# Two experts' 64-row remainders put into one shared 128-row tile in a tokeniser, attention and expert kernel

## The reference

```python
cap = int(CAP_FACTOR * B * S / E)          # 1.25 * 2048 / 8 = 320
idx = argmax(softmax(t @ Wr));  pos = rank of the token within its expert
kept = pos < cap
disp[idx * cap + pos] = t                  # (8 * 320, 256), kept tokens only
h = relu(ein[e] @ W1[e])                   # 320 x 256 @ 256 x 1024
eout = h @ W2[e]                           # 320 x 1024 @ 1024 x 256
comb = kept ? eout[flat] : t;  out = comb * (kept ? pmax : 1)
result = layernorm(t + out)
```

## Time and profile before

| | before |
|---|---|
| median of 3 runs | 245.89 us (245.63 to 246.35) |
| the profiled execution's own time | 245.8 us |
| its span | 244.1 us |
| PE busy | 230.0 us, 94% of the span |
| DVE / ACT / POOL busy | 185.3 / 152.2 / 96.6 us |
| mean granted TensorE clock | 0.989 |
| DMA | 35.88 MB, mean 147 GB/s |

### The profile page before, as it was taken

One profiled execution on the slowest core, in us unless ns is written; L12 is line 12 of the kernel. 1 busy time (PEld: TensorE's weight loads), 2 busy tenths in 40 slices (PEclk: granted clock), 3 DMA queues, 4 the chain that ended last, 5 costly groups with the idle time before them and its releaser, 6 DMA issues.

```text
span 244.1 us, 5000 instructions
## 1 busy us (share of the span) xinstructions
PE 230.0 (94%) x1670; PEld 222.3 (91%) x1670; DVE 185.3 (76%) x558; ACT 152.2 (62%) x355; POOL 96.6 (40%) x170
## 2 busy tenths in 40 slices
PE   6999999999999999889999999999999999999940
PEld 5999999999999998658999999999999999999940
DVE  6878797787979798897676767967779677789550
ACT  5336567786877887466675676674766757666100
POOL 7001228474665656557000025232262322623672
PEclk9999999999999999999999999999999999999995
DMA  5925975083796020301899919064090650100100
GB/s 169 299 74 178 284 234 151 26 237 151 238 394 228 6 83 3 85 0 50 245 352 361 349 48 359 3 214 167 12 379 10 201 176 3 48 0 24 36 4 0
DMA packets 28666, 35.88 MB, mean 147 GB/s; under 512 B 2684, under 2 KB 25579, under 8 KB 28642
## 3 DMA queue, kind: packets, MB, share of 16 engines
q1 hardware_dynamic: 26434, 32.11, 40.8%
q0 software_dynamic: 1792, 3.47, 3.9%
q10 hardware_dynamic: 416, 0.00, 0.1%
HBM read 27.37 MB, written 9.47 MB: 151 GB/s over the span
## 4 chain that ended last, share of the span: by engine, by line
PE 85%; issue 4%; POOL 4%; DVE 3%; ACT 2%; POOLq 1%; DMA 0%; ACTq 0%; DVEq 0%
PE bank L1329 16%; PE bank L1330 15%; PE bank L1331 15%; PE bank L1400 14%; PE bank L1417 5%; PE bank L1454 5%; POOL out_dram L589 3%; PE bank L1586 2%; PE bank L1470 2%; PE bank L1636 2%; PE bank L1494 2%; PE bank L1428 2%; PE bank L1472 1%; PE bank L1471 1%; POOL yrstd L613 1%
## 5 line engine op out<-in xcount | busy, mean ns | idle before, releaser
L1243 DVE SCALAR_TENSOR_TENSOR h_lo<-bank,h_hi 128x320 fp32r<-128x320 f32 x58 | 28.3, 490 | 24.7 <-ACT h_hi L854 21.9
L854 ACT ACTIVATE h_hi<-bank 128x320 fp32r<-128x320 f32 x58 | 25.4, 438 | 34.6 <-PE bank L1331 34.6
L1329 PE MATMUL bank<-einT_hi,w_hi 128*128 128x320 f32 x128 | 40.3, 315 | 0.2 <-DVE einT_lo L1235 0.2
L1331 PE MATMUL bank<-einT_hi,w_lo 128*128 128x320 f32 x128 | 39.6, 309 | 0.0
L1330 PE MATMUL bank<-einT_lo,w_hi 128*128 128x320 f32 x128 | 39.5, 309 | 0.0
L589 POOL DMA_INDIRECT out_dram<-tokens_mem,images x24 | 27.7, 1155 | 29.3 <-ACT tokens_mem L871 22.2
L992 DVE TENSOR_TENSOR w_lo<-w_raw,w_hi 128x1024 fp32r<-128x1024 f32 x32 | 38.9, 1216 | 0.0
L1329 PE MATMUL bank<-h_hi,w_hi 128*128 128x320 f32 x112 | 35.1, 313 | 0.0
L1330 PE MATMUL bank<-h_lo,w_hi 128*128 128x320 f32 x112 | 34.6, 309 | 0.0
L1331 PE MATMUL bank<-h_hi,w_lo 128*128 128x320 f32 x112 | 34.6, 309 | 0.0
L771 ACT ACTIVATE w_hi<-w_raw 128x1024 fp32r<-128x1024 f32 x32 | 33.7, 1054 | 0.0
(11 more groups left out here) (235 smaller groups left out, 570.9 us busy)
## 6 DMA issues: line engine op xcount, KB each, us to landing
w_raw<-in_L_ffn_W_dram SPq DMA_DIRECT2D x16, 1024.0 KB, 8.0
images<-in_x_dram SPq DMA_DIRECT2D x7, 768.0 KB, 5.1
dispatched<-blank SPq DMA_DIRECT2D x4, 645.0 KB, 9.6
images<-dispatched SPq DMA_DIRECT2D x6, 387.0 KB, 9.2
out_dram<-lone SPq DMA_DIRECT2D x8, 256.0 KB, 7.7
images<-dispatched SPq DMA_DIRECT2D x3, 258.0 KB, 4.4
images<-in_x_dram SPq DMA_DIRECT2D x2, 384.0 KB, 5.3
out_dram<-tokens_mem,images POOLq DMA_INDIRECT x24, 3.5
```

The costliest lines, as they stand in the source:

```text
L854: act.activation(hidden_halves(n)[0], hidden_bank(n)[:, 0:CAP], ACT.Relu).then_inc(h_hi_ready, 1)
L1243: dve.scalar_tensor_tensor(lo, hidden_bank(n)[:, 0:CAP], 0.0, hi.bitcast(F32), ALU.max, ALU.subtract).then_inc(h_ready, 1)
L1329: pe.matmul(to, ah, bh, start=first, stop=False)
L1331: return pe.matmul(to, al, bh, start=False, stop=last)
```

## The change

For experts 1 to 6 (`PAIRED`) an odd expert and the even one behind it share a tile. The odd expert's load is unchanged: its third tile `ein[:, e, 2, :]` holds its last 64 rows and the next expert's first 64. The even expert loads two tiles only, from its row 64 on. For an odd expert `ein_t` turns three tiles as before, but into another order of columns, and the shared tile with an identity whose halves are swapped (`ident_swapped`), so that the odd expert's 320 columns stand at 64 to 383 and the even one's first 64 at 0 to 63, where they stay. The even expert turns its two tiles into columns 64 to 319. On the way out, `sums` is 384 columns wide; the odd expert stores at 0 (its last 64 columns first) and turns back two tiles of 128, the even expert stores at 64 and turns back three tiles of 128, the first of them the shared one. Sums, statistics, normalisation and scatter follow the tiles: two tiles for experts 1, 3, 5 and three full ones for experts 2, 4, 6. Experts 0 and 7 keep 128, 128, 64. The POOL queue's third scatter of expert 5 (it stood behind the power for expert 6) is gone. At the start POOL fills a wider identity and makes one more select.

The core of the diff:

```diff
@@ -57,6 +57,8 @@
     NS = len(SLOTS)
+    HALF = P // 2
+    PAIRED = range(1, E - 1)
     SCALE = float(D) ** -0.5
@@ -76,7 +78,8 @@
-        ident = sb("ident", [P, P])
+        ident_wide = sb("ident_wide", [P, HALF + P])
+        ident, ident_swapped = ident_wide[:, HALF:HALF + P], ident_wide[:, 0:P]
         causal = sb("causal", [P, S])
@@ -205,13 +208,56 @@
         h_lo = sb("h_lo", [P, 3, CAP], F32R)
-        sums = sb("sums", [P, DC, CAP])
+        sums = sb("sums", [P, DC, CAP + HALF])
...
         def pick(b, s):
-            return sums[:, s, :] if b == B - 1 else tokens_mem[:, s * CAP:(s + 1) * CAP]
+            return sums[:, s, 0:CAP] if b == B - 1 else tokens_mem[:, s * CAP:(s + 1) * CAP]
+
+        def shares_first(e):
+            return e in PAIRED and e % 2 == 1
+
+        def tiles_of(e):
+
+            if e not in PAIRED:
+                return [(j, n) for j, (_, n) in enumerate(SLOTS)]
+            return [(0, P), (1, P)] if shares_first(e) else [(0, P), (1, P), (2, P)]
+
+        def tile_columns(e):
+
+            return slice(0, NS - 1) if shares_first(e) else slice(0, NS)
+
+        def rows_tile(e, j):
+            if e in PAIRED and e % 2 == 0 and j == 0:
+                return ein[:, e - 1, NS - 1, :]
+            return ein[:, e, j, :]
+
+        def tiles_ahead(e):
+            return sum(len(tiles_of(i)) for i in range(e))
+
+        def scatters_ahead(e):
+
+            return sum(len(tiles_of(i)) for i in range(e % 2, e, 2))
+
+        def sums_at(e):
+            return 0 if shares_first(e) or e not in PAIRED else HALF
+
+        def turned_at(e, j):
+            if e not in PAIRED:
+                return TURNED[j]
+            return ((2, 0), (2, D), (6, 0))[j if shares_first(e) else j - 1]
+
+        def turned_from(e, j):
+            if e not in PAIRED:
+                return SLOTS[j][0]
+            if shares_first(e):
+                return HALF + j * P
+            return P + (j - 1) * P if j else 0
+
+        def einT_at(e):
+            return HALF if shares_first(e) else 0
@@ -358,10 +404,11 @@
                 full = CAP // P
-                if 0 < e < E - 1:
-                    sp.dma_start(ein[:, e, :, :],
-                                 dispatched[e * CAP:e * CAP + NS * P].rearrange("(j p) r -> p j r", p=P)
-                                 ).then_inc(ein_in[e], 16)
+                if e in PAIRED:
+                    first, o = (0, 0) if shares_first(e) else (1, HALF)
+                    sp.dma_start(ein[:, e, first:NS, :],
+                                 dispatched[e * CAP + o:e * CAP + o + (NS - first) * P].rearrange(
+                                     "(j p) r -> p j r", p=P)).then_inc(ein_in[e], 16)
                     return
@@ -424,7 +471,7 @@
                 sp.wait_ge(lone_out[i], 16 * (B // 2))
-                sp.wait_ge(z_out[i], 16 * NS * (E // 2))
+                sp.wait_ge(z_out[i], 16 * scatters_ahead(E + i))
@@ -452,9 +499,11 @@
             step(pool.memset(avg[:, :], 1.0 / D))
-            link(pool.memset(ident[:, :], 0.0))
+            link(pool.memset(ident_wide[:, :], 0.0))
             pool.affine_select(out=ident[:, :], in_=ident[:, :], compare_op=ALU.not_equal, fill=1.0,
                                base=0, pattern=[[-1, P]], channel_multiplier=1).then_inc(pool_const, 1)
+            step(pool.affine_select(out=ident_wide[:, 0:HALF], in_=ident_wide[:, 0:HALF], compare_op=ALU.not_equal,
+                                    fill=1.0, base=-HALF, pattern=[[-1, HALF]], channel_multiplier=1))
             link(pool.memset(blank[:, :], 0.0))
@@ -580,14 +629,16 @@
                     pool.wait_ge(z_ready, e - 1)
-                link(pool.tensor_tensor(yrstd[:, e % 2], yve[:, :], minus_half[:, 0:NS], ALU.pow))
-                pool.tensor_tensor(ynmr[:, e % 2], ynmean[:, :], yrstd[:, e % 2], ALU.mult).then_inc(yrstd_ready, 1)
+                c = tile_columns(e)
+                link(pool.tensor_tensor(yrstd[:, e % 2, c], yve[:, c], minus_half[:, c], ALU.pow))
+                pool.tensor_tensor(ynmr[:, e % 2, c], ynmean[:, c], yrstd[:, e % 2, c], ALU.mult
+                                   ).then_inc(yrstd_ready, 1)
...
-                n = SLOTS[j][1]
+                n = dict(tiles_of(e))[j]
                 pool.indirect_dma_start(
-                    out_rows, bass.IndirectOffsetOnAxis(ap=ein[0:n, e, j, D + 1:D + 2].bitcast(U32), axis=0),
+                    out_rows, bass.IndirectOffsetOnAxis(ap=rows_tile(e, j)[0:n, D + 1:D + 2].bitcast(U32), axis=0),
                     z[0:n, e % 2, j, :], None, bounds_check=T - 1, oob_is_err=False
@@ -597,7 +648,7 @@
                 pool.wait_ge(z_ready, e + 1)
-                for j in range(NS):
+                for j, _ in tiles_of(e):
                     scatter_tile(e, j)
@@ -618,10 +669,9 @@
             pool.wait_ge(z_ready, E - 2)
-            scatter_tile(E - 3, 0)
-            scatter_tile(E - 3, 1)
+            for j, _ in tiles_of(E - 3):
+                scatter_tile(E - 3, j)
             scale_late(0)
-            scatter_tile(E - 3, 2)
             scatter_late(0)
@@ -844,7 +894,8 @@
                     act.wait_ge(einT_done, DC * e + c + 1)
-                    act.activation(einT_hi[:, e % 2, c, :], bank[b][:, 0:CAP], ACT.Copy).then_inc(einT_hi_ready, 1)
+                    act.activation(einT_hi[:, e % 2, c, :], bank[b][:, einT_at(e):einT_at(e) + CAP], ACT.Copy
+                                   ).then_inc(einT_hi_ready, 1)
@@ -861,13 +912,14 @@
                         act.wait_ge(h_used, FC * (e + 1))
-                    act.activation(sums[:, c, :], bank[SUM_BANKS[c]][:, 0:CAP], ACT.Copy).then_inc(sum_ready, 1)
+                    act.activation(sums[:, c, sums_at(e):sums_at(e) + CAP], bank[SUM_BANKS[c]][:, 0:CAP], ACT.Copy
+                                   ).then_inc(sum_ready, 1)
...
                 if e >= 2:
-                    act.wait_ge(z_out[e % 2], 16 * NS * (e // 2))
-                for j, (_, n) in enumerate(SLOTS):
+                    act.wait_ge(z_out[e % 2], 16 * scatters_ahead(e))
+                for j, n in tiles_of(e):
                     ins = act.activation(z[0:n, e % 2, j, :], y[0:n, e % 2, j, :], ACT.Identity,
@@ -1232,7 +1284,7 @@
                     dve.wait_ge(einT_hi_ready, DC * e + c + 1)
-                    ins = dve.tensor_tensor(einT_lo[:, e % 2, c, :], bank[b][:, 0:CAP],
+                    ins = dve.tensor_tensor(einT_lo[:, e % 2, c, :], bank[b][:, einT_at(e):einT_at(e) + CAP],
                                             einT_hi[:, e % 2, c, :].bitcast(F32), ALU.subtract)
@@ -1250,32 +1302,34 @@
                     dve.wait_ge(ein_in[0], 64)
-                for j, (_, n) in enumerate(SLOTS):
-                    at, o = TURNED[j]
+                for j, n in tiles_of(e):
+                    at, o = turned_at(e, j)
+                    rows = rows_tile(e, j)
                     dve.scalar_tensor_tensor(y[0:n, e % 2, j, :], bank[at][0:n, o:o + D],
-                                             ein[0:n, e, j, D:D + 1], ein[0:n, e, j, 0:D],
+                                             rows[0:n, D:D + 1], rows[0:n, 0:D],
                                              ALU.mult, ALU.add).then_inc(y_ready, 1)
...
             def expert_stats(e):
-                for j, (_, n) in enumerate(SLOTS):
-                    dve.wait_ge(y_ready, NS * e + j + 1)
+                for i, (j, n) in enumerate(tiles_of(e)):
+                    dve.wait_ge(y_ready, tiles_ahead(e) + i + 1)
                     step(dve.bn_stats(ystats[0:n, j, :], y[0:n, e % 2, j, :]))
...
                 settle()
-                for j, (_, n) in enumerate(SLOTS):
+                c = tile_columns(e)
+                for j, n in tiles_of(e):
                     step(dve.bn_aggr(ymv[0:n, j, :], ystats[0:n, j, :]))
...
                 if e < E - 2:
-                    step(dve.tensor_scalar(ynmean[:, :], ymv[:, :, 0], -1.0, None, ALU.mult))
+                    step(dve.tensor_scalar(ynmean[:, c], ymv[:, c, 0], -1.0, None, ALU.mult))
                     settle()
-                dve.tensor_scalar(yve[:, :], ymv[:, :, 1], EPS, None, ALU.add).then_inc(yvar_ready, 1)
+                dve.tensor_scalar(yve[:, c], ymv[:, c, 1], EPS, None, ALU.add).then_inc(yvar_ready, 1)
...
-                n = SLOTS[j][1]
+                n = dict(tiles_of(e))[j]
                 dve.tensor_scalar(z[0:n, e % 2, j, :], y[0:n, e % 2, j, :], ymv[0:n, j, 0:1],
@@ -1297,7 +1351,7 @@
                             dve.wait_ge(yrstd_ready, e)
-                            dve.wait_ge(z_out[(e - 1) % 2], 16 * NS * ((e - 1) // 2))
+                            dve.wait_ge(z_out[(e - 1) % 2], 16 * scatters_ahead(e - 1))
                             for i in range(NS):
@@ -1307,13 +1361,13 @@
             e = E - 1
-            dve.wait_ge(z_out[e % 2], 16 * NS * (e // 2))
+            dve.wait_ge(z_out[e % 2], 16 * scatters_ahead(e))
             for j, (_, n) in enumerate(SLOTS):
```

(24 more changed lines are left out.)

## The result

| | before | after |
|---|---|---|
| median | 246.53 us (245.63 to 246.89, 6 runs) | 243.97 us (243.88 to 244.57, 6 runs) |
| ratio after / before, 95% interval | | 0.9907 (0.989 to 0.9924), or 1.9 to 2.7 us less |
| the same kernel on a second occasion (run e1) | 246.03 us | 244.39 us, ratio 0.9926 (0.9907 to 0.9945), or 1.4 to 2.3 us less |
| profiled execution, its span | 245.8, 244.1 us | 243.94, 242.2 us |

The change is faster, as forecast, and the time lies in the range. The two profiled executions differ by 1.9 us, and so do their spans.

A forecast was written before the change was run, and what follows sets the result against it. PE was taken to bound the expert stage, a POOL and DVE relay the end. Savings of 1.32 + 0.30 = 1.62 us from 245.89 gave 244.3 us, range 243.7 to 245.0.

The forecast's parts named there:

- PE is the bound of the expert stage and the price is the spacing: Expert stage: PE waits for nobody, so 12 fewer transposes at 0.11 us spacing save 1.32 us.
- The 3.3 us estimated from it: Expert stage, rival: each of 12 transposes saves its full record of 272 ns, 3.26 us, total time 242.3; chance 0.01.
- The end gives 0.30 us by a change of releaser: End: POOL's power for expert 6 waits for `yve` instead of two scatters, starting at 225.32 instead of 225.62.
- PE's wait: Near the end, PE's wait for DVE's low half of a hidden block falls from 0.36 to 0.06 us.
- The wide scatter costs 0, bounds 0.1: End: the scatter of expert 6's third tile, 128 rows instead of 64, costs 0, bounds -0.1 and +0.1 us.
- The third scatter of expert 5 buys nothing: End: this scatter leaves POOL's queue ahead of a 1.27 us wait, so it adds nothing beyond what is counted.
- Loads and cover: Expert stage: smaller loads lie beside PE, and ACT and DVE hand back hidden blocks in time; cost zero.
- The rest costs nothing: Start and elsewhere: POOL's wider fill and extra select, at most 0.2 + 0.3 us, hide beside a 14.61 us wait.
- The sum: Whole kernel: 1.32 us from PE plus 0.30 us at the end, 1.62 us less.

The follow-up runs named there:

- e2: Changed kernel with the 12 removed transposes put back on PE as dummies nobody reads; ratio 0.9974 to the kernel before.
- e9: Changed kernel with 36 dummy transposes on PE, six in each of six blocks; ratio 1.0089 to the kernel before.
- e3: Changed kernel with only experts 5 and 6 sharing a tile, 1 to 4 as before the change; ratio 0.9974 to the kernel before.
- e4: Changed kernel with only experts 1 to 4 sharing tiles, and POOL's old order at the end; ratio 0.9963 to the kernel before.
- e6: Kernel before, with ACT reporting expert 5 after its second tile and POOL's third scatter waiting for its own flag; ratio 0.9993.
- e7: Changed kernel with the scatter of expert 6's third tile moved ahead of POOL's power for expert 7's first tile; ratio 0.9911 to the kernel before.
- e8: As e7, with DVE taking expert 7's third tile before normalising the second, and POOL's last power before the second tile's scatter; ratio 0.9878 to the kernel before.
- e5: Changed kernel with even experts loading three tiles again, the shared one unused; ratio 0.9934 to the kernel before.
- e12: Changed kernel with three more scatters that write nothing, one each behind those of experts 1, 2 and 3; ratio 0.9938 to the kernel before.
- e10: Kernel before with only the wider identity added: 64 more columns filled and a second select on POOL; ratio 1.0008.

## Why the prediction was right, and what it missed

- *PE is the bound of the expert stage and the price is the spacing.* Right: 1.28 us for the predicted 1.32, gone with 12 dummies (e2), linear up to 36 (e9), divided by pairs as counted (e3, e4). The Trainium skill's 275 ns (TensorE: Matmul & The Clock Gate, Part 4: PE-mode transpose) is again the length of the record, 272 ns here. The 3.3 us estimated from it are excluded by e2 and e9.
- *The end gives 0.30 us by a change of releaser.* Right, and e6 shows it alone at the predicted 225.32, with 0.32 us in the relay. PE's wait is gone where 0.06 us was forecast. The relay's 0.20 in place of 0.30 is mostly the wide scatter.
- *The wide scatter costs 0, bounds 0.1.* 0.08 in its old place (1.17 for 1.09), inside the bounds. In the place of e7 and e8, away from DVE's normalisation, 128 rows take 0.97. So the 64 more rows cost 0.08 us in one place, and the place makes 0.20.
- *The third scatter of expert 5 buys nothing.* Right up to the last scatter (e6), and its loss opened the room that e7 uses. Wrong behind it: it is one of the three scatters whose 0.08 us each left POOL's `DRAIN`.
- *Loads and cover.* Right: PE stays at 106.00 of 106.00 us, and e5 shows no part of the loads.
- *The rest costs nothing.* This step failed twice, both times by little. The stretch behind the last scatter was taken as fixed, and shrank by 0.25 us with three scatters fewer (e12). And POOL's wider fill and select were held against POOL's own wait, while they lengthen two DVE instructions by 0.18 us (e10).
- *The sum.* 1.28 + 0.20 + 0.25 = 1.73 us between the profiles, against 1.62. That it came so close is in part luck: the two terms of the sum were 0.14 us too large together, and 0.25 us came from a place that was taken as fixed. The last scatter's start at 237.90, forecast as about 237.9, is luck too: 0.15 us of it are the earlier start of this execution. The rest of the measured 1.8 to 2.3 is inside the intervals and the start's own variation of 1.3 us; the runs show no other cause and rule none out of that size.

## What to carry to other kernels

Where an engine is busy without a gap, price an instruction by the distance to its neighbour in a block, not by its record, and count how many go in the code; that gave 1.32 for 1.28 us. Where an engine waits, ask who arrives next when the late one leaves, and look for what fits into the idle time that opens: the reordered end shortened the relay by another 1.0 us. Compare stretches between marks rather than spans when the start varies more than the effect. And look at what runs behind the last counted instruction: here a `DRAIN` on POOL ends the program, and fewer output scatters shorten it, also those of experts long done.

## What the runs showed that I had not expected

- The time from the start of the last scatter to the end of the span follows the number of output scatters of the whole execution: 4.28 us with 21 (eight profiles; 4.25 in the two where the last scatter itself takes 0.91 us and not 0.94), 4.36 with 22, 4.44 with 23, 4.53 with 24 (four profiles, one of them with three scatters that write nothing). From the end of the last scatter to the end of POOL's `DRAIN` it is 3.11, 3.19, 3.27 and 3.35 us, 0.08 for each scatter. POOL also issues 16 scatters into `dispatched`, between 40 and 113 us; 3.11 us over 37 and 3.35 over 40 are both 0.084. So it is an estimate that this stretch takes 0.084 us for each indirect DMA of the whole program. No run changed the 16, and what POOL does in the `DRAIN` is open.
- 64 more columns to fill and a select of 64 columns on POOL lengthened two DVE instructions beside them from 0.63 to 0.81 us. An exclusive lock on a port pair that DVE and GpSimd share would do this. The Trainium skill (page SBUF - State Buffer, section SBUF: two separate sides) states such a lock for DVE instructions in a 2-port mode or with two SBUF inputs; the rows show the delay, not the port or the mode.
